# Router logits with stationary weights, and parked value operands split on VectorE, in a fused decoder-block kernel

## The chip, the core and the metric

The kernel runs on one NeuronCore of a Trainium2 chip. Its engines are TensorE (PE; loads of its stationary operand are listed apart, as PEld), VectorE (DVE), ScalarE (ACT), GpSimd (POOL) and SyncE (SP), which only issues DMAs; ACT and POOL issue some too. The metric is the device time of one execution in microseconds, lower is better.

## The reference, cut to what matters

The program is two layers over 16 x 128 tokens of width 512 (2048 tokens). Two of its parts are touched here: the mixture of experts of layer 0 and the value projection of layer 1's attention.

```python
ht = h.reshape(-1, d)                       # 2048 tokens x 512
logits = ht @ router_w                      # router_w: 512 x 8
probs = jax.nn.softmax(logits, axis=-1)
topv, topi = jax.lax.top_k(probs, K)        # K = 2 of 8 experts
...
sh = jax.nn.silu(ht @ sw_gate) * (ht @ sw_up) @ sw_down
...
v_img = (img_ctx @ vi_w + vi_b).reshape(B, -1, H, D)
```

## The kernel before

Products that need full precision are made in one of two ways. Most go through `three_passes` (L101 to L105): each operand is split into a lead, rounded to the format that TensorE takes in one pass, and a trail, which is the rest; three matmuls (lead by lead, lead by trail, trail by lead) make the product. The router logits do not: they are plain float32 matmuls. The profile lists every float32 matmul that is no transpose as two records, so the 64 matmuls of L1558 are 128 records.

The work is a sequence of phases with a barrier between them. Two phases are touched.

**Phase "shared"** (`turned_and_shared`). The 2048 tokens are four groups g of 512. For each group DVE writes the normalised rows (`stage_rows`, L1457), PE turns them in four column chunks c of 128 (`turn_rows`, L1550, four transposes a chunk), ACT moves each turned chunk out of PSUM twice, as `plain` and as `lead` (`turned_rows`, L1428 and L1429), and DVE makes the trail (L1470). `plain` has one buffer a chunk for all groups: ACT may write chunk c of group g only when the router's matmul over chunk c of group g-1 has been done. `route(g)` (L1558) takes 128 tokens of a chunk as the stationary operand (128x128) and streams the 8 router columns through it; so for each chunk there are four matmuls with 8 moving columns, and the logits come out with tokens on partitions. ACT keeps them (`keep_logits`, L1434). PE's order is turn 0, turn 1, route 0, turn 2, route 1, turn 3, route 2, route 3, and then the shared expert: `up(0)`, `up(1)`, `down_product(0)` and so on, all with 512 moving columns. When all logits are kept, DVE and ACT choose the experts (L1278 to L1329), PE counts in between (`counts`, L1335 and L1336, queued inside `up(0)` after 36 of its 48 matmuls), and POOL scatters the rows by indirect DMAs (L1486).

**Phase "routed"** (`routed_experts`). In its second half 39 tiles of 128 rows go through the experts' down projections. For each tile SP loads the hidden values, ACT makes their lead (`hidden_lead`, L1901), DVE their trail (`hidden_trail`, L1967, output `routed_ht`), PE does six matmuls (`down_product`), ACT copies the result out (L1910), and SP stores it. The loop over tiles is a hardware loop on DVE (`second`). Beside it POOL prepares operands for work that was deferred to the next phase, the "parked" ones: three sets k of four pieces of 128x512 (one of turned context, two of value weights). `park(k)` issues four loads behind waits on `down`, the count of finished tiles, and `cut_parked(k)` splits them: four TENSOR_SCALAR for the leads (L1810), then four TENSOR_TENSOR for the trails (L1814). PE uses the first products of them (32 + 32 + 32 matmuls in all) from the end of this phase on.

Of the kernel before, what the change touches and what calls it, by code (L numbers as in the profile page):

```python
# [16 lines left out]
F32 = mybir.dt.float32  # L17
# [3 lines left out]
ALU = mybir.AluOpType  # L21
# [6 lines left out]
C = D // P  # L28
GB = 4
# [1334 lines left out]
def turned_and_shared(nc, K, R, E1, lead, trail, normal, logits, rows_dram, gate_up_dram, rk, rk_dram):  # L1364
# [5 lines left out]
    with Phase(nc, "shared") as ph:  # L1370
# [7 lines left out]
        square = sb("square", [P, GB])  # L1378
        ms_done, rms_done, own_late = sem("ms_done"), sem("rms_done"), sem("own_late")
# [36 lines left out]
        def _(act):  # L1416
# [4 lines left out]
            def turned_rows(g):  # L1421
                for c in chunks(g):
# [8 lines left out]

            def keep_logits(g):
                act.wait_ge(logit_mm, (g + 1) * C)
# [12 lines left out]

# [94 lines left out]
        def _(pe):  # L1541
            def turn_rows(g):
                pe.wait_ge(staged, g + 1)
                for c in chunks(g):
# [9 lines left out]
            def route(g):  # L1554
                for k, c in enumerate(chunks(g)):
                    pe.wait_ge(lead_done, through(g, c))
                    for b in range(GB):
                        ins = nc.tensor.matmul(logit_bank(g)[:, b * E:(b + 1) * E], plain[:, c, b * S:(b + 1) * S],  # L1558
                                               E1.rw[:, c, :], start=(k == 0 and b == 0), stop=(k == C - 1 and b == GB - 1))
                    ins.then_inc(logit_mm, 1)  # L1560

            def up(u):
                cols = slice(u * N, (u + 1) * N)
                for f in range(FC):
                    if u:
                        pe.wait_ge(hid_done, 2 * u + f - 1)
                    else:
                        pe.wait_ge(logit_done, 3)
                    for bank, at in ((2 * f, 0), (2 * f + 1, UP)):
                        for c in range(C):  # L1570
                            w = slice(at + c * F + f * P, at + c * F + (f + 1) * P)
# [23 lines left out]
            turn_rows(0)  # L1595
            turn_rows(1)
# [14 lines left out]
def routed_experts(nc, K, R, E1, rows_dram, hid_dram, y_dram, weights, parked, parked_raw, ct_dram, v_w):  # L1611
# [10 lines left out]
    with Phase(nc, "routed") as ph:  # L1622
# [34 lines left out]
        parked_loaded = [sem(f"parked_loaded{k}") for k in range(1 + len(DEFERRED))]  # L1657
# [103 lines left out]
        def _(pool):  # L1761
# [40 lines left out]
            def park(k):  # L1802
                for c in range(C):
                    pool.wait_ge(down, 1 + k * 5 + c)
                    pool.dma_start(parked_raw[:, k, 1, c], parts[k][c]).then_inc(parked_loaded[k], 16)

            def cut_parked(k):
                pool.wait_ge(parked_loaded[k], 16 * C)
                for c in range(C):
                    nc.gpsimd.tensor_scalar(parked[:, k, 0, c], parked_raw[:, k, 1, c], 1.0, None, ALU.mult  # L1810
                                            ).then_inc(parked_lead, 1)
                for c in range(C):
                    pool.wait_ge(parked_lead, k * C + c + 1)
                    nc.gpsimd.tensor_tensor(parked[:, k, 1, c], parked_raw[:, k, 1, c],  # L1814
                                            parked[:, k, 0, c].bitcast(F32), ALU.subtract).then_inc(parked_trail, 1)
# [115 lines left out]
        def _(dve):  # L1931
# [63 lines left out]
            second(dve, hidden_trail, skip=2)  # L1995
# [1013 lines left out]
```

## Time and profile before

| what | value |
|---|---|
| median of 3 runs | 1477.15 us (1473.38 to 1482.09) |
| profiled execution, time | 1477.78 us |
| its span in the trace | 1476.1 us |
| busy: PE, DVE, ACT, POOL | 93%, 56%, 52%, 30% |
| mean granted TensorE clock | 0.953 of 2.4 GHz |
| router stage: first turn to the last logit matmul | 536.4 to 572.3 us |
| second half of "routed", tiles 10 to 23 | 806 to 844 us |

The span is cut into 40 slices of 36.9 us in the page; in a windows view each stretch has the busy time of every engine with the number of records, then the granted clock (1.00 is 2.4 GHz, 0.50 is 1.2 GHz), the busy share of the DMA engines and GB/s. A timeline row is start, duration (from the first start to the last end where several were merged), engine, line, operation, tiles, count, and in brackets the idle time of the engine before it with what ended it.

### The profile page before, as it was taken

To read this page: it belongs to the slowest core of one execution; us is meant where nothing else is said; L and a number is where in the kernel's file an instruction comes from. 1 tells how busy PE (TensorE), PEld (TensorE's weight loads), DVE (VectorE), ACT (ScalarE), POOL (GpSimd) and SP (SyncE) were. 2 spreads that over 40 slices of the span, in tenths; PEclk is the share of its full clock that TensorE was granted. 3 is DMA by queue.
4 is the path that set the end of the run, shared out by engine and by line. 5 is a ranking of instruction groups with operands and counts; after the bars stand their busy time and mean duration, and the time that the engine had idled before them with its cause. 6 is when DMAs were issued, how large, how long until landed. Compare 5 with 4: busy or idle time off the path is not lost. (4 is left out here: it accounts for less than half of the span.)

```text
span 1476.1 us, 24769 instructions
## 1 busy us (share of the span) xinstructions
PE 1366.5 (93%) x7406; PEld 1138.8 (77%) x7407; DVE 833.3 (56%) x1530; ACT 765.8 (52%) x1878; POOL 441.4 (30%) x411
## 2 busy tenths in 40 slices
PE   6899997999999879989998698999977999999998
PEld 5786676888788768868886476888866888888887
DVE  2443433476776775354444627754228877777866
ACT  3313234787878644134555254555438566665661
POOL 0110103354747300639923824211025400000032
PEclk9999995999999976999999799999989999999999
DMA  6998448887788401466657467655535555555413
GB/s 230 358 350 305 173 144 258 292 272 257 243 277 287 151 22 36 167 208 186 204 137 243 165 230 240 178 168 186 185 128 157 166 156 163 159 163 161 136 44 114
DMA packets 172983, 284.14 MB, mean 192 GB/s; under 512 B 30112, under 2 KB 64672, under 8 KB 172640
## 3 DMA queue, kind: packets, MB, share of 16 engines
q1 hardware_dynamic: 147088, 227.58, 48.7%
q0 software_dynamic: 8672, 29.37, 6.1%
q10 hardware_dynamic: 17136, 26.09, 4.8%
q8 instruction: 47, 0.77, 0.2%
q14 instruction: 40, 0.33, 0.1%
HBM read 176.29 MB, written 106.70 MB: 192 GB/s over the span
## 5 line engine op out<-in xcount | busy, mean ns | idle before, releaser
L2646 ACT ACTIVATE attend_prob<-banks,attend_row,rq 128x128 f32<-128x128 f32 x256 | 113.9, 455 | 51.9 <-DVE attend_row L2721 51.9
L103 PE MATMUL banks<-of_shared_split,heads_wl 128*128 128x512 f32 x256 | 108.8, 425 | 11.8 <-ACT heads_ksq L949 7.2
L103 PE MATMUL banks<-attend_wol,attend_ol 128*128 (+1 forms) x256 | 105.9, 414 | 0.0
L105 PE MATMUL banks<-of_shared_split,heads_wt 128*128 128x512 f32 x256 | 103.1, 403 | 0.0
L104 PE MATMUL banks<-of_shared_split,heads_wl 128*128 128x512 f32 x256 | 103.0, 402 | 0.0
L105 PE MATMUL banks<-attend_wol,attend_ot 128*128 (+1 forms) x256 | 100.6, 393 | 0.0
L103 PE MATMUL banks<-of_shared_split,of_ctx_lead 128*128 128x512 f32 x224 | 92.1, 411 | 9.1 <-DVE of_ctx_trail L425 5.3
L103 PE MATMUL banks<-queries_rows_split,queries_wl 128*128 128x512 f32 x256 | 100.4, 392 | 0.0
L105 PE MATMUL banks<-queries_rows_split,queries_wt 128*128 128x512 f32 x256 | 99.7, 389 | 0.0
L104 PE MATMUL banks<-attend_wot,attend_ol 128*128 (+1 forms) x256 | 99.7, 389 | 0.0
L104 PE MATMUL banks<-queries_rows_split,queries_wl 128*128 128x512 f32 x256 | 99.6, 389 | 0.0
L2628 POOL TENSOR_TENSOR x_kept<-x_kept,attend_tern_bias 128x512 f32<-128x512 f32 x12 | 15.5, 1294 | 264.4 <-ACT of_attend_raw L2684 262.8
L2336 DVE TENSOR_TENSOR queries_total<-queries_total,queries_sq 128x512 f32<-128x512 f32 x60 | 41.5, 692 | 86.9 <-ACT queries_sq L2264 86.9
L2260 ACT ACTIVATE queries_head<-banks,queries_bias 128x512 f32<-128x512 f32 x64 | 44.1, 689 | 87.6 <-PE banks L105 85.6
L105 PE MATMUL banks<-of_shared_split,of_ctx_trail 128*128 128x512 f32 x224 | 89.4, 399 | 0.0
L104 PE MATMUL banks<-of_shared_split,of_ctx_lead 128*128 128x512 f32 x224 | 88.8, 396 | 0.0
L897 ACT ACTIVATE heads_dec<-mlstm_gmax,mlstm_nat 128x128 f32<-128x128 f32 x264 | 83.2, 388 | 5.8 <-POOL mlstm_gmax L799 5.8
L1058 DVE TENSOR_TENSOR heads_total<-heads_total,heads_ksq 128x512 f32<-128x512 f32 x64 | 55.9, 874 | 53.6 <-ACT heads_ksq L949 53.5
L2659 ACT ACTIVATE attend_ol<-banks,of_attend_vbias 128x512 fp32r<-128x512 f32 x64 | 44.1, 689 | 69.5 <-PE banks L2851 69.5
L2745 DVE TENSOR_TENSOR x_kept<-x_kept,banks 128x512 f32 (+1 forms) x64 | 43.9, 686 | 61.4 <-PE banks L105 61.2
L1163 PEld LDWEIGHTS banks<-heads_ctx,heads_cmat 128*128 128x128 f32 x512 | 71.8, 209 | 8.6 <-POOL heads_ctx L808 3.1
L2832 PE MATMUL banks<-attend_kn,attend_q 128*128 128x128 f32 x512 | 69.8, 281 | 5.2 <-DMA attend_q<-q_heads 5.2
(353 smaller groups left out, 3707.5 us busy)
## 6 DMA issues: line engine op xcount, KB each, us to landing
mlstm_gmax<-running_max SPq DMA_DIRECT2D x36, 512.0 KB, 6.4
heads_raw<-in_L_xattn_ki_w SPq DMA_DIRECT2D x32, 512.0 KB, 6.6
k_heads<-heads_key ACTq DMA_DIRECT2D x64, 256.0 KB, 4.6
q_heads<-queries_head SPq DMA_DIRECT2D x64, 256.0 KB, 3.0
attend_q<-q_heads SPq DMA_DIRECT2D x64, 256.0 KB, 4.1
of_attend_k<-k_heads SPq DMA_DIRECT2D x60, 256.0 KB, 4.0
of_attend_v<-v_heads SPq DMA_DIRECT2D x60, 256.0 KB, 3.3
sorted_rows<-values_zeros SPq DMA_DIRECT2D x2, 5120.0 KB, 18.2
```

The lines of the kernel that those rows point to most:

```text
L103: nc.tensor.matmul(out, lead_l, lead_r, start=first, stop=False)
L104: nc.tensor.matmul(out, lead_l, trail_r, start=False, stop=False)
L105: return nc.tensor.matmul(out, trail_l, lead_r, start=False, stop=last)
L897: ins = nc.scalar.activation(dec[:, n % 2, b], gmax[:, h // 2 % 4, h % 2 * N + b * S:h % 2 * N + (b + 1) * S], ACT.Exp, scale=-1.0, bias=M ...
L1058: nc.vector.tensor_tensor(t, t, ksq[:, m % 2, :], ALU.add).then_inc(total_done, 1)
L1163: ins = nc.tensor.matmul(ps[:, n // 2 % 2, at:at + DH0 + 1], cmat[:, n % RING, b, :], ctx1[:, bass.ds(half(g), 1), b, n, :].rearrange("p a ...
L2260: nc.scalar.activation(head[:, u % HEADS_RING, :], ps[:, u % 4, :], ACT.Identity, bias=bias[:, h:h + 1]).then_inc(head_done, 1)
L2336: nc.vector.tensor_tensor(t, t, sq[:, u % 2, :], ALU.add).then_inc(total_done, 1)
L2646: ins = nc.scalar.activation(prob[:, j % 2, b, :], ps[:, j % 2, b * S:(b + 1) * S], ACT.Exp, bias=row[:, j % 2, 1, b:b + 1], scale=rq[:, b ...
L2659: nc.scalar.activation(ol[:, par, j, :], ps[:, 4 + j % 2, :], ACT.Identity, bias=vbias[:, bass.ds(quad_of(it) * 4 + j, 1)]).then_inc(ol_do ...
L2745: nc.vector.tensor_tensor(xb, xb, ps[:, 6 + b % 2, :], ALU.add).then_inc(acc_done, 1)
L2832: ins = nc.tensor.matmul(ps[:, j % 2, s], q[:, j, s], kn[:, j % 2, s], start=True, stop=True)
```

## The change

Two edits, in two phases.

In "shared", `route(g)` takes the 8 router columns of a chunk as the stationary operand (128x8) and streams all 512 tokens: one matmul a chunk, four a group. The logits then lie across, 8 partitions by 512 tokens. ACT copies them to SBUF (`keep_across`), four small transposes turn them upright (`upright_logits`) into the same bank, and `keep_logits` waits for those. The order on PE and ACT changes round this: the last chunk of a group is turned after the route of the group before; the uprights of groups 2 and 3 are put inside `up(0)`, after its first six matmuls.

In "routed", POOL only issues the twelve parked loads, piece by piece, one for every 2.5 tiles (`down` counts 1, 3, 6, 8, ... 28). DVE splits them: for a piece one TENSOR_SCALAR behind the hidden trail of tile 9 + 5*piece//2, and one TENSOR_TENSOR behind the next tile's. DVE's loop over tiles is written out.

```diff
@@ shared: ScalarE
+            def keep_across(g):
+                act.wait_ge(logit_mm, (g + 1) * C)
+                nc.scalar.activation(across[:, g % 2, :], logit_bank(g)[0:E, :], ACT.Copy).then_inc(across_done, 1)
...
-            turned_rows(0)
-            turned_rows(1)
-            keep_logits(0)
-            turned_rows(2)
-            keep_logits(1)
-            turned_rows(3)
-            keep_logits(2)
-            keep_logits(3)
+            first, rest = slice(0, 1), slice(1, C)
+            turned_rows(0, slice(0, C))
+            turned_rows(1, slice(0, C))
+            for g in range(2, G):
+                keep_across(g - 2)
+                turned_rows(g, first)
+                keep_logits(g - 2)
+                turned_rows(g, rest)
+            keep_across(G - 2)
+            keep_across(G - 1)
+            keep_logits(G - 2)
+            keep_logits(G - 1)
@@ shared: TensorE
-                    for b in range(GB):
-                        ins = nc.tensor.matmul(logit_bank(g)[:, b * E:(b + 1) * E], plain[:, c, b * S:(b + 1) * S],
-                                               E1.rw[:, c, :], start=(k == 0 and b == 0), stop=(k == C - 1 and b == GB - 1))
-                    ins.then_inc(logit_mm, 1)
+                    nc.tensor.matmul(logit_bank(g)[0:E, :], E1.rw[:, c, :], plain[:, c, :], start=k == 0, stop=k == C - 1
+                                     ).then_inc(logit_mm, 1)
+
+            def upright_logits(g):
+                pe.wait_ge(across_done, g + 1)
+                for b in range(GB):
+                    ins = nc.tensor.transpose(logit_bank(g)[:, b * E:(b + 1) * E], across[:, g % 2, b * S:(b + 1) * S],
+                                              K.ident[0:E, 0:E])
+                ins.then_inc(upright, 1)
...
+                            if u == 0 and f == 0 and at == 0 and c == 2:
+                                upright_logits(G - 2)
+                                upright_logits(G - 1)
...
-            turn_rows(2)
-            route(1)
-            turn_rows(3)
-            route(2)
-            route(3)
+            for g in range(2, G):
+                turn_rows(g, slice(0, C - 1))
+                upright_logits(g - 2)
+                route(g - 1)
+                turn_rows(g, slice(C - 1, C))
+            route(G - 1)
@@ routed: GpSimd
-            park(0)
-            for k in range(1, len(parts)):
-                park(k)
-                cut_parked(k - 1)
-            cut_parked(len(parts) - 1)
-            pool.wait_ge(parked_trail, len(parts) * C)
+            for piece in range(PIECES):
+                k, c = divmod(piece, C)
+                pool.wait_ge(down, 1 + 5 * piece // 2)
+                pool.dma_start(parked_raw[:, k, 1, c], parts[k][c]).then_inc(parked_loaded[piece], 16)
@@ routed: VectorE
-            second(dve, hidden_trail, skip=2)
+            def parked_piece(piece, part):
+                k, c = divmod(piece, C)
+                if part == 0:
+                    dve.wait_ge(parked_loaded[piece], 16)
+                    nc.vector.tensor_scalar(parked[:, k, 0, c], parked_raw[:, k, 1, c], 1.0, None, ALU.mult
+                                            ).then_inc(parked_lead, 1)
+                else:
+                    dve.wait_ge(parked_lead, piece + 1)
+                    nc.vector.tensor_tensor(parked[:, k, 1, c], parked_raw[:, k, 1, c],
+                                            parked[:, k, 0, c].bitcast(F32), ALU.subtract).then_inc(parked_trail, 1)
+
+            PARTS = {9 + 5 * piece // 2 + part: (piece, part) for piece in range(PIECES) for part in range(2)}
+            for n in range(2, TILES):
+                hidden_trail((n // 8, n % 8))
+                if n in PARTS:
+                    parked_piece(*PARTS[n])
+            dve.wait_ge(parked_trail, PIECES)
```

TensorE's program from the first turned rows to the shared expert, before (`of_x_normal` are the normalised rows, `of_ffn_raw` holds `plain`, `of_shared_rw` is the router's weight):

```order
L1550 MATMUL banks<-ident,of_x_normal 128x128 x32
L1558 MATMUL banks<-of_shared_rw,of_ffn_raw 128x8 x16
L1550 MATMUL banks<-ident,of_x_normal 128x128 x16
L1558 MATMUL banks<-of_shared_rw,of_ffn_raw 128x8 x16
L1550 MATMUL banks<-ident,of_x_normal 128x128 x16
L1558 MATMUL banks<-of_shared_rw,of_ffn_raw 128x8 x32
```

The same place now (`shared_hid` holds the logits that lie across):

```order
L1560 MATMUL banks<-ident,of_x_normal 128x128 x32
L1567 MATMUL banks<-of_ffn_raw,of_shared_rw 8x512 x4
L1560 MATMUL banks<-ident,of_x_normal 128x128 x12
L1573 MATMUL banks<-ident,shared_hid 128x8 x4
L1567 MATMUL banks<-of_ffn_raw,of_shared_rw 8x512 x4
L1560 MATMUL banks<-ident,of_x_normal 128x128 x16
L1573 MATMUL banks<-ident,shared_hid 128x8 x4
L1567 MATMUL banks<-of_ffn_raw,of_shared_rw 8x512 x4
L1560 MATMUL banks<-ident,of_x_normal 128x128 x4
L1567 MATMUL banks<-of_ffn_raw,of_shared_rw 8x512 x4
```

The 64 narrow router matmuls have become 16 wide ones; one chunk of groups 2 and 3 is turned behind a route, and four uprights stand ahead of routes 1 and 2.

VectorE's program in the second half of "routed", before, from the third tile to the head of its loop:

```order
L1967 TENSOR_TENSOR routed_ht<-routed_ring,routed_hl 128x256 x2
L1967 TENSOR_TENSOR routed_ht<-routed_lead,routed_hl 128x256 x4
L1967 TENSOR_TENSOR routed_ht<-routed_ring,routed_hl 128x256 x4
L1967 TENSOR_TENSOR routed_ht<-routed_lead,routed_hl 128x256 x3
```

The same place now, up to the third parked piece:

```order
L1970 TENSOR_TENSOR routed_ht<-routed_ring,routed_hl 128x256 x2
L1970 TENSOR_TENSOR routed_ht<-routed_lead,routed_hl 128x256 x4
L1970 TENSOR_TENSOR routed_ht<-routed_ring,routed_hl 128x256 x2
L2002 TENSOR_SCALAR parked<-parked_raw 128x512
L1970 TENSOR_TENSOR routed_ht<-routed_ring,routed_hl 128x256
L2006 TENSOR_TENSOR parked<-parked_raw,parked 128x512
L1970 TENSOR_TENSOR routed_ht<-routed_ring,routed_hl 128x256
L2002 TENSOR_SCALAR parked<-parked_raw 128x512
L1970 TENSOR_TENSOR routed_ht<-routed_lead,routed_hl 128x256
L2006 TENSOR_TENSOR parked<-parked_raw,parked 128x512
L1970 TENSOR_TENSOR routed_ht<-routed_lead,routed_hl 128x256 x2
L2002 TENSOR_SCALAR parked<-parked_raw 128x512
```

Each parked piece is two instructions behind two tiles' trails; there are 12 pieces, and the last tile has none behind it.

## Rows read from the trace of the kernel before

**Rows 1.** The page: granted TensorE clock in tenths, in 40 slices.
```profile
PEclk9999995999999976999999799999989999999999
```

**Rows 2.** Windows of the router stage: busy of PE, PEld, DVE, ACT, POOL, clock, DMA.
```profile
536.40:539.20 2.80, 2.72 (x13) 2.75 (x14) 2.33 (x7) 1.53 (x3) 0.00 (x0) 0.50 0.00 0
541.30:545.00 3.70, 3.70 (x35) 3.64 (x33) 3.23 (x7) 3.66 (x7) 0.00 (x0) 1.00 0.02 4
548.30:572.20 23.90, 23.81 (x113) 23.44 (x113) 6.98 (x12) 10.19 (x18) 0.00 (x0) 0.50 0.00 1
572.30:576.90 4.60, 4.60 (x12) 3.63 (x13) 3.04 (x28) 4.12 (x6) 0.00 (x0) 0.50 0.73 213
577.00:582.00 5.00, 5.00 (x23) 4.04 (x22) 4.03 (x34) 0.60 (x1) 0.00 (x0) 1.00 0.03 9
```

**Rows 3.** Timeline of PE's weight loads in the router stage.
```profile
541.29 3.65 PEld L1558 LDWEIGHTS banks<-of_shared_rw,of_ffn_raw 128*128 128x128 f32 x32
545.01 1.34 PEld L1550 LDWEIGHTS banks<-ident,of_x_normal 128*128 128x128 f32 x12
...
548.09 6.95 PEld L1558 LDWEIGHTS banks<-of_shared_rw,of_ffn_raw 128*128 128x128 f32 x32
```

**Rows 4.** Timeline of ACT in the router stage.
```profile
537.67 0.69 ACT L1428 ACTIVATE of_ffn_raw<-banks,of_ffn_wcol 128x512 f32<-128x512 f32 x1 [3.05 <-PE banks L1550]
...
547.02 0.25 ACT L1434 ACTIVATE of_x_logits<-banks 128x32 f32<-128x32 f32 x1
551.81 0.69 ACT L1428 ACTIVATE of_ffn_raw<-banks,of_ffn_wcol 128x512 f32<-128x512 f32 x1 [4.53 <-issue]
```

**Rows 5.** Timeline of PE in an earlier phase: wide float32 matmuls, small transposes.
```profile
116.66 3.65 PE L557 MATMUL banks<-mlstm_gmax,values_w_gate 128*64 128x512 f32 x8
120.24 0.51 PE L103 MATMUL banks<-of_shared_split,of_ctx_lead 128*128 128x512 f32 x1
...
133.26 0.43 PE L569 MATMUL banks<-ident,values_irow 32*128 32x32 f32 x4 [1.30 <-DVE of_ffn_raw L462]
```

**Rows 6.** Timeline at the expert choice: DVE's marks, PE's counts.
```profile
579.52 0.29 DVE L1295 TENSOR_TENSOR shared_both<-shared_chosen 128x128 f32<-128x128 f32 x1
...
582.84 0.38 PE L1335 MATMUL banks<-shared_both,shared_before 128*128 128x128 f32 x2
```

**Rows 7.** Timeline of DVE in the second half of "routed".
```profile
796.37 0.43 DVE L1967 TENSOR_TENSOR routed_ht<-routed_lead,routed_hl 128x256 fp32r<-128x256 f32 x1 [2.11 <-ACT routed_hl L1901]
...
805.95 1.22 DVE L1967 TENSOR_TENSOR routed_ht<-routed_ring,routed_hl 128x256 fp32r<-128x256 f32 x1 [1.07 <-ACT routed_hl L1901]
...
812.70 5.65 DVE L1967 TENSOR_TENSOR routed_ht<-routed_lead,routed_hl 128x256 fp32r<-128x256 f32 x2 [0.90 <-ACT routed_hl L1901]
...
844.15 0.43 DVE L1967 TENSOR_TENSOR routed_ht<-routed_lead,routed_hl 128x256 fp32r<-128x256 f32 x1 [2.31 <-ACT routed_hl L1901]
...
867.39 0.43 DVE L1967 TENSOR_TENSOR routed_ht<-routed_lead,routed_hl 128x256 fp32r<-128x256 f32 x1 [1.15 <-ACT routed_hl L1901]
```

**Rows 8.** Timeline of POOL there, and the parked loads' time to landing.
```profile
812.37 4.94 POOL L1814 TENSOR_TENSOR parked<-parked_raw,parked 128x512 fp32r<-128x512 f32 x4
...
DMA to landing us min/median/max: 3.7/5.2/6.3
```

**Rows 9.** Waits of PE from 806 to 842: us in total, times, longest.
```profile
PE banks L103 <- DVE routed_ht L1967: 13.2, 5, 5.1
```

**Rows 10.** Windows of the second half of "routed", and of the barrier behind it.
```profile
806.00:844.15 38.15, 24.81 (x79) 17.89 (x78) 24.80 (x13) 11.78 (x27) 35.50 (x29) 0.81 0.58 203
...
794.00:806.00 12.00, 11.55 (x46) 8.27 (x47) 2.86 (x8) 6.20 (x15) 3.02 (x6) 1.00 0.93 302
872.60:874.40 1.80, 0.01 (x1) 0.00 (x1) 0.00 (x0) 0.01 (x1) 0.00 (x0) 1.00 0.00 0
```

**Rows 11.** Groups of DVE instructions: count, busy us, mean ns.
```profile
L1470 DVE TENSOR_TENSOR of_x_trail<-of_ffn_raw,of_x_lead 128x512 fp32r<-128x512 f32 x16 | 10.9, 692 | 14.6 <-ACT of_x_lead L1429 14.6
L1457 DVE TENSOR_SCALAR of_x_normal<-x_kept,mv,of_shared_scale 128x512 f32<-128x512 f32 x16 | 7.9, 555 | 0.0
```

More of the change, by code:

```diff
@@ L1378, in turned_and_shared @@
         square = sb("square", [P, GB])
+        across = hid[0:E]
+        across_done, upright = sem("across_done"), sem("upright")
         ms_done, rms_done, own_late = sem("ms_done"), sem("rms_done"), sem("own_late")
@@ L1419, in _, with turned_rows @@
             act.wait_ge(E1.small_loaded, 32)
-            def turned_rows(g):
-                for c in chunks(g):
+            def turned_rows(g, at):
+                for c in chunks(g)[at]:
                     bank = ps[:, 4 * (g % 2) + c, :]
@@ L1430, in turned_rows @@
                                          ).then_inc(lead_done, 1)
+            def keep_across(g):
+                act.wait_ge(logit_mm, (g + 1) * C)
+                nc.scalar.activation(across[:, g % 2, :], logit_bank(g)[0:E, :], ACT.Copy).then_inc(across_done, 1)
             def keep_logits(g):
-                act.wait_ge(logit_mm, (g + 1) * C)
+                act.wait_ge(upright, g + 1)
                 nc.scalar.activation(logits[:, g * GB:(g + 1) * GB, :],
@@ L1541, in _, with turn_rows @@
         def _(pe):
-            def turn_rows(g):
+            def turn_rows(g, at):
                 pe.wait_ge(staged, g + 1)
-                for c in chunks(g):
+                for c in chunks(g)[at]:
                     if g >= 2:
@@ L1566, in up @@
                         pe.wait_ge(hid_done, 2 * u + f - 1)
-                    else:
-                        pe.wait_ge(logit_done, 3)
                     for bank, at in ((2 * f, 0), (2 * f + 1, UP)):
+                        if u == 0 and f == 0 and at:
+                            pe.wait_ge(logit_done, 3)
                         for c in range(C):
+                            if u == 0 and f == 0 and at == 0 and c == 2:
+                                upright_logits(G - 2)
+                                upright_logits(G - 1)
                             w = slice(at + c * F + f * P, at + c * F + (f + 1) * P)
@@ L1594, in _ @@
             pe.wait_ge(E1.small_loaded, 32)
-            turn_rows(0)
-            turn_rows(1)
+            turn_rows(0, slice(0, C))
+            turn_rows(1, slice(0, C))
             route(0)
-            turn_rows(2)
-            route(1)
-            turn_rows(3)
-            route(2)
-            route(3)
+            for g in range(2, G):
[4 more added lines that the diff above has]
+            route(G - 1)
             pe.wait_ge(trail_done, G * C)
@@ L1656, in routed_experts @@
         held_act, held_sp = sem("held_act"), sem("held_sp")
-        parked_loaded = [sem(f"parked_loaded{k}") for k in range(1 + len(DEFERRED))]
+        PIECES = (1 + len(DEFERRED)) * C
+        parked_loaded = [sem(f"parked_loaded{k}") for k in range(PIECES)]
         parked_lead, parked_trail, parked_product = sem("parked_lead"), sem("parked_trail"), sem("parked_product")
@@ L1800, in _ @@
             parts += [[v_w[c * P:(c + 1) * P, q * N:(q + 1) * N] for c in range(C)] for q, _ in DEFERRED]
[L1802 to L1815, printed above, removed]
-            park(0)
-            for k in range(1, len(parts)):
-                park(k)
-                cut_parked(k - 1)
-            cut_parked(len(parts) - 1)
-            pool.wait_ge(parked_trail, len(parts) * C)
+            for piece in range(PIECES):
+                k, c = divmod(piece, C)
+                pool.wait_ge(down, 1 + 5 * piece // 2)
+                pool.dma_start(parked_raw[:, k, 1, c], parts[k][c]).then_inc(parked_loaded[piece], 16)
         @block.scalar
```

## The prediction

> **What bounds the kernel now.** PE is busy 93% of the span, so I looked for the places where it is slow or stands. First the clock in 40 slices [rows 1]: most are 9; below it are the 7th (5) and the 31st (8), which the change does not touch, the 15th and 16th (7 and 6; 517 to 590 us) and the 23rd (7; 812 to 849 us). The two edits lie on these.
>
> *Router stage.* The windows [rows 2] show PE busy all the time, but from 548.3 to 572.2 at clock 0.50, that is 1.2 GHz; before, from 541.3 to 545.0, the same work ran at 2.4 GHz. The weight loads give the price [rows 3]: 16 router matmuls (32 records) took 3.65 us at full clock and 6.95 at half. Just before the clock fell PE had been doing this narrow work; it came back only after 4.6 us of the shared expert's wide matmuls [rows 2]. ACT waited 4.53 us for the slow route [rows 4], so PE bounds the stage.
>
> *Second half of "routed".* The DVE timeline [rows 7] lets one count tiles: from the trail of tile 10 (805.95) to that of tile 23 (844.15) are 13 tiles in 38.2 us, 2.94 each. From tile 23 to the last, tile 38 (867.39), are 15 in 23.24 us, 1.55 each; from tile 4 (796.37) to tile 10, six in 9.58 us, 1.60 each. In between one sees why: the trail that starts at 812.70 and its successor take 5.65 us where two take 0.85, and over the first of them lie POOL's four TENSOR_TENSOR, 4.94 us from 812.37 [rows 8]. PE waited for these trails 13.2 us in five waits [rows 9], and the whole stretch ran at clock 0.81 instead of 1.00 [rows 10]: after each long wait the clock was at half for some microseconds.
>
> **Edit 1, the parked operands.** It removes POOL's 24 splitting instructions, so nothing holds DVE's trails. At the neighbours' pace the 13 tiles take 13 x 1.55 = 20.2 us instead of 38.2, that is 18.0 less; tile 24 followed tile 23 still at half clock, which is about 1 us more (six matmuls of 0.22 us at full clock [rows 2], twice that at half). Gain 19.0 us. Ends: at 1.60 a tile 17.4 and no such 1 us; at 1.48 (the 15 tiles without that 1 us) 20.0.
>
> What it adds to DVE: 12 TENSOR_SCALAR, nearest row 0.56 us, and 12 TENSOR_TENSOR, nearest row 0.69 us [rows 11], one behind a tile's trail: 15 us in all. Their cover is DVE's wait for ACT in each tile, 1.07 to 1.15 us at full pace [rows 7]. 0.69 fits with some 0.4 left, so I take zero. Without that cover all 15 would lie on the path, since PE queues behind the trail; that is the upper end. Splitting instructions also wait for their load. Load k is issued when tile 1+k has been finished and used behind the trail of tile 9+k, which DVE makes about a tile ahead of PE: some 7 tiles, 11 us. The load landed in 3.7 to 6.3 us [rows 8], with the DMA engines at 0.93 [rows 10], and now the loads come one in 2.5 tiles and not bunched. So nothing waits. The last piece is cut behind tile 37, before PE needs it. POOL's wait on `down` holds nothing behind it but the next load.
>
> **Edit 2, the router.** Prices. A float32 matmul with 512 moving columns: four of them (8 records) stand between 116.66 and 120.24 [rows 5], 0.895 us each at full clock. 16 make 14.3 us, 3.58 a group, against 3.65 before at the same clock: so the edit saves nothing by the amount of work, only by the clock, if wide streams hold it up. Transposes: 12 in 1.34 us, 0.112 each [rows 3]. Four uprights: 0.43 us by four small transposes [rows 5]. ACT's pair for a chunk: eight pairs from 537.67 to 547.02, 1.17 each; so 0.6 for the copy across, which has as many columns, and 0.2 for keeping the upright ones [rows 4].
>
> The schedule by these, with the clock at 2.4 GHz, from where ACT ends its eighth pair (547.0). ACT copies across to 547.6; PE, which ended turn 2's three chunks at 546.3, makes the uprights to 548.1 and route 1 to 551.7. ACT may start group 2 when route 1's second matmul frees its chunk (549.9) and ends it, with one keep of 0.2, at 554.8; across to 555.4. PE ends turn 3's chunks at 553.5 and stands 2 us for that copy: a new wait. Uprights to 555.9, route 2 to 559.5, last chunk of turn 3 to 559.95. ACT's group 3 goes from 556.9 to 561.7; route 3 follows it closely and ends at 563.5. Before it was 572.2: 8.7 us less.
>
> Then the shared expert: it started with 4.6 us at half clock; at full clock 2.3 less. Inside `up(0)` come eight uprights, 0.9 more. The logits are now complete some 2.5 us after `up(0)` begins instead of 0.3. DVE needs 7.1 us from there to the counted marks (572.7 to 579.8 [rows 6]), so they come at +9.6; PE reaches the counts after 36 matmuls of 0.22 to 0.23 [rows 2] and the uprights, at +9.0: 0.6 us of wait, where it had 3 us to spare. The scatters start at about the same distance from `up(0)` as before, so nothing later is touched. Sum with the clock up: -8.7 - 2.3 + 0.9 + 0.6 = -9.5.
>
> The clock is the open point. At half clock a wide matmul costs 1.79 us, twice. What speaks for it staying up: the wide float32 matmuls of [rows 5] ran inside a dense stretch at full clock; the 1.8 us of idleness at a barrier left it at 1.00 [rows 10]; and turning alone, 2.8 us from 536.4, was enough to raise it (half there, full at 541.3, where the first route begins [rows 2, 3]). Against: the stage now has two pauses of 1.4 and 2 us, next to uprights that are as narrow as the old router matmuls. I reckon with one fall. It halves the speed of one route until wide work has raised it: route 2 would end at about 561.2 instead of 559.5, and the stage at 565.3, 1.8 us later. So edit 2 gives -9.5 with none, -7.7 with one; I take -8.5.
>
> The Trainium skill ("TensorE: Matmul & The Clock Gate", Part 4) says that transposes do not count as PE activity, by which the turning could never have raised the clock here; the rise with transposes alone before it says otherwise. By that rule the new stage, a third of it transposes, would tend to stay at 1.2 GHz, which is the second rival.
>
> **Sum.** The profiled execution took 1477.78 us, 0.6 above the median of the runs. 1477.8 - 19.0 - 8.5 = 1450.3; both phases end in barriers, and nothing of the later phases starts before them, so the gains stay. I predict 1450.
>
> **Rivals.**
> - *Only one of the covers holds: DVE's splitting shows.* If each of the 24 instructions delays the next trail and PE with it, by 0.2 us, 5 us are lost: 1455; all 15 would make 1465. For it: PE's slack over DVE is about half a microsecond a tile. Against: the cover of 1.1 us in every row of the quiet stretch. 0.12.
> - *The clock stays at 1.2 GHz through the router stage.* Three routes at 7.16 instead of 6.9, 16 uprights at 0.22, the shared expert's slow start as before, and the short stands for the copies: 0.8 + 3.5 + 1 = 5 us more than before instead of 8.5 less: 1478 - 19 + 5 = 1464. 0.08.
> - *Slower: the parked loads come late.* DVE's queue is in order, and a splitting instruction that waits for its load holds the trails of all later tiles. Each microsecond of landing beyond the 11 us costs one, twelve times; it makes the kernel slower when the loads take more than about 11 + 27.5/12 = 13.3 us each, and with loads of 14 us the time is 1478 - 27.5 + 36 = 1486. The rows show 6.3 at most, while DVE worked on the trails [rows 8]. The Trainium skill ("SBUF — State Buffer", "SBUF: two separate sides") says that a VectorE instruction which uses both ports of its one input, a float32 TENSOR_SCALAR among them, keeps GpSimd from writing descriptors. Here such an instruction lasts 0.56 us and comes once in 2.5 tiles, so it could add 0.56 to a landing, not 7. 0.03.
> - *Edit 1 does not do what it says:* the tiles are slow for the traffic on the DMA engines and not for POOL. Against it: PE's waits are for the trails, and the quick tiles before 806 ran at a DMA share of 0.93, the slow ones at 0.58 [rows 10]. Then only edit 2 is left: 1469. 0.04.
> - The forecast, both edits as above: 0.73.
>
> **How the numbers follow.** The forecast's own range is 1446 (1.48 a tile, no fall, no wait at the counts) to 1454 (1.60 a tile, two falls). To hold 8 in 10 the range takes in the better half of the other cases, and the spread of the runs (4 us either way): 1443 to 1461. A change of 0.5% (7.4 us) is about what this measurement can tell. All cases but the third end faster by more: faster 0.95; about the same 0.03 (two of the losses together); slower 0.02.
>
> **What would show it.** In the profile after: no POOL work from 780 us on but DMA issues; the trails at 0.42 us throughout, 1.5 to 1.6 us a tile, and no wait of PE for them; clock 1.00 from the third tile on. Router stage of about 27 us from the first turn to the last route, instead of 35.8; PE waiting for the copy across before the second set of uprights, about 2 us, and some tenths for the marks before the counts. Wrong would be: trails spaced wider just behind the splitting instructions; a clock of 0.50 through the routes; DVE waiting for a parked load.

## The result and the profile after

The changed kernel takes 1453.25 us (median; 1450.51 to 1455.23) against 1477.15 us (1473.38 to 1482.09): a ratio of 0.9832, 95% interval 0.9806 to 0.9858, or 24 us less. The profiled execution of after took 1450.51 us with a span of 1448.8. In a later comparison the same kernel gave 1450.64 and a ratio of 0.9827 (0.9793 to 0.986).

The page's line of the granted clock answers [rows 1]. The 16th slice went from 6 to 9 and the 23rd from 7 to 9. The 15th stays at 7: the first two groups are still turned at half clock in it. The 30th went from 8 to 6; it lies in a part that no edit touches.

```profile
PEclk9999996999999979999999999999969999999999
```

**Router stage.** PE's timeline, to be held against [rows 2, 3]; a row has start, duration, engine, line, operation, output and inputs, and what ended the wait before it:

```profile
534.08 6.51 PE L1560 MATMUL banks<-ident,of_x_normal 128*128 128x128 f32 x32 [6.58 <-DVE of_x_normal L1467]
540.52 3.60 PE L1567 MATMUL banks<-of_ffn_raw,of_shared_rw 128*8 128x512 f32 x8
544.05 1.53 PE L1560 MATMUL banks<-ident,of_x_normal 128*128 128x128 f32 x12
546.84 0.41 PE L1573 MATMUL banks<-ident,shared_hid 8*128 8x8 f32 x4 [1.26 <-ACT shared_hid L1436]
547.18 3.60 PE L1567 MATMUL banks<-of_ffn_raw,of_shared_rw 128*8 128x512 f32 x8
550.71 1.97 PE L1560 MATMUL banks<-ident,of_x_normal 128*128 128x128 f32 x16
554.43 0.41 PE L1573 MATMUL banks<-ident,shared_hid 8*128 8x8 f32 x4 [1.75 <-ACT shared_hid L1436]
554.77 3.60 PE L1567 MATMUL banks<-of_ffn_raw,of_shared_rw 128*8 128x512 f32 x8
558.30 0.66 PE L1560 MATMUL banks<-ident,of_x_normal 128*128 128x128 f32 x4
558.88 3.60 PE L1567 MATMUL banks<-of_ffn_raw,of_shared_rw 128*8 128x512 f32 x8
562.41 0.50 PE L103 MATMUL banks<-of_x_lead,of_shared_split 128*128 128x512 f32 x1
```

Every route (a group's four wide matmuls, eight records) lasts 3.60 us, the full-clock price, where route 1 of before took 6.95 at half clock [rows 3]. The two new waits stand where they were forecast, before the uprights, 1.26 and 1.75 us. From the first turn to the shared expert are 28.3 us, before 35.8. The windows say the same of the clock (columns: busy of PE, PEld, DVE, ACT, POOL, then clock, DMA share, GB/s):

```profile
543.00:548.00 5.00, 3.74 (x21) 1.89 (x20) 3.61 (x7) 3.79 (x7) 0.00 (x0) 1.00 0.00 0
548.00:553.00 5.00, 4.67 (x23) 2.18 (x21) 2.46 (x6) 3.85 (x8) 0.00 (x0) 1.00 0.01 3
553.00:558.00 5.00, 3.57 (x12) 0.96 (x12) 1.93 (x3) 3.50 (x8) 0.00 (x0) 1.00 0.00 0
...
796.00:838.00 42.00, 41.47 (x170) 30.44 (x169) 22.99 (x52) 25.52 (x57) 4.32 (x8) 1.00 0.93 318
```

**Second half of "routed".** The last of these windows answers [rows 10]: PE busy 41.5 of 42 us at clock 1.00, with the DMA engines at 0.93. In the DVE timeline the trails (L1970) and the new splitting (L2002, L2006) alternate, and DVE still waits for ACT before most of the trails:

```profile
795.73 0.42 DVE L1970 TENSOR_TENSOR routed_ht<-routed_ring,routed_hl 128x256 fp32r<-128x256 f32 x1 [0.68 <-ACT routed_hl L1904]
796.07 0.68 DVE L2006 TENSOR_TENSOR parked<-parked_raw,parked 128x512 fp32r<-128x512 f32 x1
797.20 0.43 DVE L1970 TENSOR_TENSOR routed_ht<-routed_ring,routed_hl 128x256 fp32r<-128x256 f32 x1 [0.44 <-ACT routed_hl L1904]
797.54 0.42 DVE L2002 TENSOR_SCALAR parked<-parked_raw 128x512 fp32r<-128x512 f32 x1
798.57 0.43 DVE L1970 TENSOR_TENSOR routed_ht<-routed_lead,routed_hl 128x256 fp32r<-128x256 f32 x1 [0.61 <-ACT routed_hl L1904]
```

The waits of [rows 9], 13.2 us in five, are gone. What is left of PE's waits for a trail between 760 and 845 us are two at the very start of the down projections (778.9 and 784.7 us), which the kernel before has too (16.4 us in seven from 760 us on, of which 3.2 are these two):

```profile
PE banks L103 <- DVE routed_ht L1970: 3.2, 2, 2.2
```

The parked loads landed in 3.6/5.2/7.3 us (least, median, most), and nothing waited for one.

To set executions side by side I use the time between landmarks of each trace. The *router stage* goes from PE's first turn to its first L103, the shared expert's first matmul; the *second half* from the first hidden trail to PE's first parked product behind the barrier. Stage and half are 35.8 and 86.7 us before, 28.3 and 66.4 after. The parts that no kernel here touches scatter by some us: what lies before the first turn took 529 to 539, what lies behind the half 602 to 607. So single profiles are compared by stretches, and whole times by medians or, between two comparisons, by the ratios to the kernel before, whose own median moved by 3 us from one to the next. The two measures differ by some us in places; then both are given.

### The profile page after: what moved, and what is told of

Read it like the earlier page. It is cut to its first block and busy times, and to the rows that moved or that the text cites. A ratio compares the mean times of both kernels' runs of the same rounds, so it can differ in the third digit from the quotient of the medians.

```text
span 1448.8 us, 24581 instructions
## 1 busy us (share of the span) xinstructions
PE 1351.7 (93%) x7326; PEld 1115.2 (77%) x7327; DVE 831.5 (57%) x1554; ACT 767.9 (53%) x1882; POOL 407.4 (28%) x387
## 5 line engine op out<-in xcount | busy, mean ns | idle before, releaser
L103 PE MATMUL banks<-of_shared_split,heads_wl 128*128 128x512 f32 x256 | 107.5, 420 | 11.1 <-ACT heads_ksq L949 6.0
L103 PE MATMUL banks<-attend_wol,attend_ol 128*128 (+1 forms) x256 | 105.9, 414 | 0.0
L103 PE MATMUL banks<-of_shared_split,of_ctx_lead 128*128 128x512 f32 x224 | 92.9, 415 | 9.2 <-DVE of_ctx_trail L425 5.2
L103 PE MATMUL banks<-queries_rows_split,queries_wl 128*128 128x512 f32 x256 | 100.5, 392 | 0.0
L2355 DVE TENSOR_TENSOR queries_total<-queries_total,queries_sq 128x512 f32<-128x512 f32 x60 | 41.5, 692 | 86.8 <-ACT queries_sq L2283 86.8
```

Of the source, the lines that this page charges most:

```text
L103: nc.tensor.matmul(out, lead_l, lead_r, start=first, stop=False)
```

## The experiments

All ran beside the kernel before: the first four with its median at 1474.77 us (15 runs), the next four at 1473.76 (25 runs), the last three at 1476.46 (11 runs).

### One edit at a time

The first kernel has the router edit alone (the parked code of before), the second the parked edit alone (the router code of before).

> Only the router edit; the parked operands are split by GpSimd as before. My theory: the router stage ends about 7.6 us earlier after its first turn and the shared expert starts at full clock, so 1477 - 8.5 = 1468.5 (1466 to 1471), with clock 1.00 through all four routes and the three long waits for routed_ht still there (13 us). Rival (the clock in the profiled execution was luck): the clock falls in one of the two pauses in this execution, and the gain is 5 us or less, 1472 or more.

> Only the parked edit; the router is as before. My theory: 13 tiles at 1.47 to 1.5 us instead of 2.94, and 1 us behind them: 1477 - 19.5 = 1457.5 (1455 to 1460). PE's waits for routed_ht fall from 13.2 us to none. If the two edits add up, the two gains of this run and of the router alone make 24 to 28 us. Rival (the two edits share a gain): this one alone already gives 1453.

Router alone: 1467.44 us (10 runs), ratio 0.9947 [0.9931 to 0.9964], 7.8 us less by the ratio. Parked alone: 1458.15 (6 runs), ratio 0.9889 [0.9867 to 0.9911], 16.4 us less. Together 24.2, which is what the change gains: within these intervals the edits add up.

The router-only trace did not keep the clock up in all four routes, as its theory had it: route 2 lasts 5.30 us, 1.7 more than the others. The gain was there all the same, and not the 5 us or less of the rival; its stage is 28.5 us. The parked-only trace has the narrow router in a second execution: stage 37.8 us, 2 more than before, with the clock down already in route 0 and no wait of PE after the first turn. PE's waits for a trail are the two at the start there, 3.2 us.

In the router-only trace the old rows are all there, 15.2 us in six, of which 4.7 in two are those of the start. PE's waits from 760 us to the end of the half, the trails on DVE, and GpSimd over them:

```profile
PE banks L103 <- DVE routed_ht L1986: 15.2, 6, 4.1
```

```profile
801.20 5.62 DVE L1986 TENSOR_TENSOR routed_ht<-routed_lead,routed_hl 128x256 fp32r<-128x256 f32 x2 [0.90 <-ACT routed_hl L1920]
```

```profile
800.85 4.94 POOL L1833 TENSOR_TENSOR parked<-parked_raw,parked 128x512 fp32r<-128x512 f32 x4
```

### What in the router kept the clock down: streaming little

This kernel undoes the router edit but for one thing: in the old form, tokens stationary, the eight router columns are streamed 16 times over. The logits are the same, only read with a stride. No copy across, no uprights, the old order.

```diff
-        ins = nc.tensor.matmul(logit_bank(g)[:, b * E:(b + 1) * E], plain[:, c, b * S:(b + 1) * S],
-                               E1.rw[:, c, :], ...)
+        ins = nc.tensor.matmul(logit_bank(g)[:, b * 16 * E:(b + 1) * 16 * E], plain[:, c, b * S:(b + 1) * S],
+                               E1.rw[:, c, :].unsqueeze(1).broadcast_to([P, 16, E]), ...)
```

> The parked edit, and the router as before in form and order: 128 tokens stationary, 64 matmuls; only the 8 router columns are streamed 16 times over (128 moving columns, 15 of 16 results unread). Weight loads are unchanged, and the longer stream (4 x 128 columns at 2.4 GHz are some 0.22 us by the 0.895 us of 512) fits under them. Theory (the loss was the clock alone, and it fell because PE streamed only 8 columns at a time): the clock stays at 1.00, each route takes 3.7 us, and the router stage is as short as with the change or up to 3 us shorter, for it has no copy across and no uprights: 1450 to 1454. Rival 1 (the clock follows the form of the work, loads of 128 columns against streams, and not how much is streamed): clock 0.50 through routes 1 to 3, time as with the parked edit alone, 1457 or more. Rival 2 (streams do not fit under the loads): clock 1.00 but routes of 5 us and more.

1448.0 us (6 runs), ratio 0.9826 [0.9798 to 0.9854]; stage 26.5 us. The time is 2 us better than the range of the theory, the stage within it. The comparison that isolates the columns is the one with the parked-only kernel, on the same chip: the two differ in nothing else, the time falls from 1458.15 us, with intervals of the ratios that do not touch, and the stage from 37.8. In the parked-only kernel the turning and the routing of a group from 539.41 us on went so:

```profile
539.41 3.65 PE L1550 MATMUL banks<-ident,of_x_normal 128*128 128x128 f32 x16
542.86 6.83 PE L1558 MATMUL banks<-of_shared_rw,of_ffn_raw 128*128 128x8 f32 x32
```

With the columns repeated:

```profile
544.48 0.63 PE L1550 MATMUL banks<-ident,of_x_normal 128*128 128x128 f32 x4 [1.07 <-ACT of_x_logits L1434]
544.94 3.74 PE L1558 MATMUL banks<-of_shared_rw,of_ffn_raw 128*128 128x128 f32 x32
548.52 1.47 PE L1550 MATMUL banks<-ident,of_x_normal 128*128 128x128 f32 x12
551.95 0.63 PE L1550 MATMUL banks<-ident,of_x_normal 128*128 128x128 f32 x4 [1.96 <-ACT of_x_logits L1434]
552.41 7.31 PE L1558 MATMUL banks<-of_shared_rw,of_ffn_raw 128*128 128x128 f32 x64
```

The same 32 weight loads take 3.74 us a group, as the 8-column form did at full clock (3.65, [rows 3]), and two groups in a row 7.31, so the clock no longer falls. The old form was not slow by itself: it hid its streaming under the weight loads, streamed next to nothing, and was then given half the clock. Sixteen times as many columns cost 0.09 us a group.

### How many columns, and in which order

Two more versions with repeated columns use a new order on PE, the route ahead of the last chunk's transposes:

```diff
 turn_rows(0); turn_rows(1); route(0)
-turn_rows(2); route(1); turn_rows(3); route(2); route(3)
+for g in range(2, G):
+    turn_rows(g, slice(0, C - 1))
+    route(g - 1)
+    turn_rows(g, slice(C - 1, C))
+route(G - 1)
```

> The kernel with the router's eight columns streamed 16 times (as in the earlier run of that name) and, besides, TensorE's program reordered there: the routing of the group before comes ahead of the last chunk's transposes, not behind them. That kernel showed two waits of TensorE for ScalarE's copy of the logits, 1.07 and 1.96 us, just ahead of that last chunk; behind 3.7 us of routing both should vanish. Theory: the stretch from the first turn to the shared expert goes from 26.5 to about 23.5 to 24.5 us, the clock stays up, and the median goes from 1448 to about 1445 to 1446. Rival (the routing then waits for ScalarE's leading parts, since ScalarE's pairs of 1.17 us are the bound of the stretch): no shorter, 26.5.

> The kernel with repeated router columns in the new order of TensorE, but with the eight columns streamed 4 times (32 moving columns) in place of 16 times (128). With 8 columns the granted clock fell to 1.2 GHz in the routing, with 128 it stayed up; the routing of a group lasted 3.65 and 3.74 us at full clock, so fewer columns save no time on TensorE. Theory A (what matters is how much the engine streams, and 32 columns are nearer to 8): the clock falls to 0.50 in part of the routing, the stretch from the first turn to the shared expert is 28 to 38 us. Theory B (32 columns suffice between the transposes): the clock stays at 1.00, 24 us, as with 128.

With 128 columns: 1444.36 us (1443.75 to 1444.89, 5 runs), ratio 0.9816 [0.9782 to 0.985], stage 24.1 us, and PE waits for nothing after the first turn. With 32 columns: 1454.32 us (4 runs), ratio 0.9851 [0.9804 to 0.9897], stage 28.0. Its clock fell twice, as these windows show, and the shared expert again began at half clock:

```profile
546.00:548.00 2.00, 2.00 (x20) 2.00 (x20) 2.00 (x5) 1.84 (x4) 0.00 (x0) 0.99 0.00 0
548.00:550.00 2.00, 2.00 (x12) 2.00 (x10) 1.24 (x3) 2.00 (x5) 0.00 (x0) 0.50 0.00 0
550.00:552.00 2.00, 2.00 (x15) 2.00 (x13) 1.16 (x2) 0.99 (x3) 0.00 (x0) 0.65 0.00 0
552.00:554.00 2.00, 2.00 (x21) 2.00 (x20) 0.50 (x1) 1.80 (x4) 0.00 (x0) 1.00 0.00 0
554.00:556.00 2.00, 2.00 (x16) 2.00 (x15) 1.07 (x3) 2.00 (x5) 0.00 (x0) 0.70 0.00 0
556.00:558.00 2.00, 2.00 (x11) 2.00 (x11) 1.20 (x2) 1.03 (x3) 0.00 (x0) 0.50 0.00 0
```

PE is busy 2.00 of 2.00 in each of them: an engine that never waits still lost its clock. That is theory A, at the short end of its stage of 28 to 38 us. Between the 32-column and the 128-column version only the number of streamed columns differs. The clocks rest on one profile each; the ratios point the same way, but their intervals overlap. (The clock had risen later in the turns of the 128-column trace, 6.59 us against 5.46; but the version before this one, also with 128 columns, had it early, two pauses besides, and no fall.)

### The pauses of the wide form

> The change with one edit: the four transposes that turn a group's logits upright stand between the second and the third wide product of the next group's routing, not ahead of the first. In the changed kernel TensorE waited 1.26 and 1.75 us ahead of these transposes for ScalarE's copy across (3.0 us over the stretch). Theory: 1.8 us of products now cover the copy; the waits vanish or shrink to under 0.5 us, unless the last chunk's transposes now wait for the copy back (up to 0.6 us each); the stretch goes from 28.3 to 25 to 26.5 us, the median 2 to 3 us below the change's. Rival (the stretch is bound by ScalarE's pairs of 1.17 us, 16 of them): it stays at 28.

```diff
 def route(g, inside=None):
     for k, c in enumerate(chunks(g)):
+        if k == 2 and inside is not None:
+            upright_logits(inside)
...
-    upright_logits(g - 2)
-    route(g - 1)
+    route(g - 1, g - 2)
```

1447.72 us (1442.35 to 1448.53, 6 runs), ratio 0.9794 [0.9759 to 0.9828]; stage 25.5. The change itself, beside it on the same chip:

> The change itself, unaltered, beside the others on one chip, so that the versions with repeated columns can be set against it. Expected: within 2 us of its median of 1453.25 us, a ratio to the kernel before of 0.983; the version with repeated columns in the new order (1444.36 us) is then some 8 to 9 us faster.

1450.64 us (1449.74 to 1453.73, 6 runs), ratio 0.9827 [0.9793 to 0.986]; stage 28.5. The ratio is the forecast one, the median 2.6 us lower than the first; so the version with 128 columns in the new order leads it by 6 us by the medians and by 2 by the ratios, and not by 8 to 9. The intervals of the two ratios overlap, but the runs on this one chip do not, and the traces show the 3 us. The waits of 1.26 and 1.75 us are gone in the version with the uprights inside:

```profile
544.04 1.88 PE L1569 MATMUL banks<-of_ffn_raw,of_shared_rw 128*8 128x512 f32 x4
545.85 0.41 PE L1575 MATMUL banks<-ident,shared_hid 8*128 8x8 f32 x4
546.19 1.88 PE L1569 MATMUL banks<-of_ffn_raw,of_shared_rw 128*8 128x512 f32 x4
```

The repeated trace of the change showed the fall of the clock that the prediction had reckoned with:

```profile
551.97 0.41 PE L1573 MATMUL banks<-ident,shared_hid 8*128 8x8 f32 x4 [1.75 <-ACT shared_hid L1436]
552.31 5.30 PE L1567 MATMUL banks<-of_ffn_raw,of_shared_rw 128*8 128x512 f32 x8
```

```profile
552.00:554.00 2.00, 2.00 (x7) 0.61 (x8) 0.24 (x1) 0.32 (x1) 0.00 (x0) 0.73 0.00 0
554.00:556.00 2.00, 2.00 (x4) 0.33 (x3) 0.69 (x1) 1.65 (x5) 0.00 (x0) 0.50 0.00 0
556.00:558.00 2.00, 2.00 (x8) 0.59 (x6) 0.69 (x1) 1.82 (x4) 0.00 (x0) 0.91 0.00 0
```

Seven profiles have this wide form with its two pauses. In five (router only, leads on GpSimd, lead six times, split earlier, the repeat) route 2 lasts 5.30 us; in two (the first profile of the change, trails on GpSimd) it lasts 3.60. In those two the clock had risen later in turns 0 and 1, which lasted 6.51 us against 5.03 to 5.64. So an execution pays once, either 0.9 to 1.5 us there or 1.7 us here, and the stages come out alike, 28.3 to 29.2. With the uprights inside, no route showed the fall, but that is one profile, in which turns 0 and 1 took 6.58; a fall averted by the missing pause is not shown by it.

### What blocked VectorE: GpSimd's operations of two inputs

Two kernels give GpSimd one half of the splitting back, one operation at a time between the loads.

> The changed kernel, but the leads of the parked pieces are made by GpSimd again (one TENSOR_SCALAR of 1.5 us a piece, spread out), the trails by VectorE. Theory (GpSimd's two-input TENSOR_TENSOR was what held VectorE for 4 to 5 us; its one-input instructions only stretch a trail from 0.42 to 0.8 us): within 2 us of the changed kernel, 1453 to 1456, trails of 0.8 us where they overlap, no wait of PE over 1 us. Rival (any GpSimd arithmetic blocks VectorE for its whole duration and puts PE behind): twelve stalls of about 1 us, 1462 or more.

> The mirror of the run with the leading parts on GpSimd: VectorE cuts the leading parts as in the change, GpSimd subtracts for the trailing ones, one at a time, spread out over the tiles and not four in a row. Theory A (a two-input operation of GpSimd holds VectorE's two-input operation for as long as it lasts, 1.2 to 1.3 us each): one or two of VectorE's trails beside each of the 12 subtractions last up to 1.3 us longer, which VectorE's idle 1.05 us mostly hides: time within 3 us of the change, stretched trails 0.43 to about 1.7 us in the trace. Theory B (it holds it through a whole batch only because four come in a row, and TensorE waits when VectorE is held for longer than about two tiles' slack): the same, and so 4.9 us stretches are gone. Rival C (any two-input subtraction on GpSimd costs several us each): 15 us slower or more, as with the kernel before.

Leads on GpSimd (TENSOR_SCALAR, one input): 1453.1 us (4 runs, 1449.55 to 1458.48), ratio 0.9848 [0.9815 to 0.9881], PE's wait for trails 3.2 us in the two at the start as in the change, half 69.5 us. A trail beside such an operation lasts 0.73 instead of 0.43 us (the first one 1.22), which the idle time hides:

```profile
808.13 0.73 DVE L1980 TENSOR_TENSOR routed_ht<-routed_lead,routed_hl 128x256 fp32r<-128x256 f32 x1 [0.98 <-ACT routed_hl L1914]
```

```profile
808.48 1.73 POOL L1825 TENSOR_SCALAR parked<-parked_raw 128x512 fp32r<-128x512 f32 x1
```

Trails on GpSimd (TENSOR_TENSOR, two inputs): 1460.73 us (10 runs), ratio 0.992 [0.9894 to 0.9947], half 77.0 us. DVE and GpSimd there:

```profile
806.80 1.90 DVE L1981 TENSOR_TENSOR routed_ht<-routed_lead,routed_hl 128x256 fp32r<-128x256 f32 x1 [2.01 <-ACT routed_hl L1915]
```

```profile
807.12 1.29 POOL L1825 TENSOR_TENSOR parked<-parked_raw,parked 128x512 fp32r<-128x512 f32 x1
```

DVE's trail had begun at 806.80, 0.3 us before GpSimd, and ended at 808.70, 0.3 us after it: its own 0.42 us, the whole 1.29 of the other, and 0.2 more. From 796 to 850 us PE waited for such trails:

```profile
PE banks L103 <- DVE routed_ht L1981: 8.0, 9, 1.2
```

The mechanism is theory A's, but its "mostly hidden" was wrong: 8.0 us of waits for 12 subtractions, 0.7 each; the time is 7 to 10 us above the change by the medians and 13 by the ratios. Four in a row, as before the change, are worse (5.1 us at a time), yet one alone already costs.

### How far the covers reach

> The change with each of the 12 leading parts that VectorE cuts of the parked pieces cut six times over, each time waiting for the one before (the same numbers are written; the result is unchanged). It prices the cover. A TENSOR_SCALAR of this size lasts 0.42 us in the changed kernel, so one piece costs VectorE 5 x 0.42 or about 2.1 to 2.6 us more, in one tile, against an idle wait for ScalarE of about 1.05 us in a tile. Theory (VectorE's splitting is free only as far as its idle time reaches): per piece 2.1 to 2.6 plus the first 0.42, less about 1.05 of that tile and some lead over TensorE, leaves 1 to 1.9 us on the path, times 12: 12 to 22 us slower than the change, about 1466 to 1475. Rival (the stage is bound by the transfers at a 0.93 share, and VectorE has slack over several tiles, which it wins back between pieces): under 4 us slower than the change.

> The change with each parked piece split behind the trail of tile 3+k instead of tile 9+k (k = 0, 2, 5, 7 ...), its load still issued when tile 1+k is finished. It prices the rival of late loads. In the changed kernel a piece is split some 12.2 us after its load's issue (782.4 to 794.6 us), and the loads land in 3.6 to 7.3 us. Six tiles of about 1.5 us earlier leave 3.2 us. Theory (VectorE's queue is in order, so a splitting instruction that waits for its load holds the trails behind it): each waits about 2 to 3 us, some 1 us of it in VectorE's idle time, 12 times: 12 to 25 us slower than the change, with VectorE shown waiting for the transfer of parked_raw. Rival (the wait is taken up by tiles finished ahead): under 4 us slower.

With each lead cut six times DVE has some 2.2 us more in every 2.5 tiles: 1464.12 us (10 runs), ratio 0.9938 [0.9912 to 0.9963], 11 to 13 us above the change by the medians and 16 by the ratios, where 12 to 22 were forecast; half 80.2 us. PE's waits from 794 to 845 us, none of which the change has:

```profile
PE banks L103 <- DVE routed_ht L1970: 10.2, 10, 1.3
```

Up to 860 us they are 12.4 us in twelve, one for each piece: of the 2.2 us, 1.2 were hidden. So DVE's slack is about one tile's idle wait, as forecast, and not several tiles'.

With the pieces split six tiles earlier DVE waits for their loads, and the time is 1459.64 us (8 runs), ratio 0.9905 [0.9876 to 0.9934], 6 to 9 us above the change by the medians and 11 by the ratios; half 74.8 us, in a profiled execution of 1454.32 us. DVE's waits from 790 to 842 us:

```profile
DVE parked L2002 <- DMA parked_raw<-in_L_xattn_vi_w: 15.0, 8, 2.7
DVE routed_ht L1970 <- ACT routed_hl L1904: 13.0, 12, 1.5
DVE parked L2002 <- DMA parked_raw<-ctx_turned: 3.6, 2, 2.3
```

PE waited 7.0 us in that stretch (794 to 842) for the trails queued behind. The mechanism is the theory's; the size, 12 to 25 us, was too high: 18.6 us of DVE's waiting reached PE as 7 in that execution, which was 5 us faster than the median.

## Why the prediction was right

The forecast of 1450 us lies 3 us below the measured 1453.25. By its own steps:

*Edit 1 takes the block away.* Right, and now shown by experiment. The trails last 0.42 to 0.43 us each, the pace from tile 10 to tile 23 is 1.47 us (13 tiles from 795.73 to 814.85) where 1.55 was taken, and the clock is 1.00. The rival that traffic was the cause is out: the loads are the same, the DMA share rose to 0.93, and the two kernels with one half of the splitting on GpSimd issue them as the change does; with the leading parts there PE's waits are as short as in the change, with the subtractions there they are back, 8.0 us.

*Its size, 19.0.* Mis-sized: the parked edit alone measured 16.4, with 17.4 as the lower end named; by its interval it may be 13 to 20. The profiles point the same way. The half lasts 86.7 and 84.5 us in the two with GpSimd's splitting as before, and 66.4 to 70.1, mean 68.6, in the eight with both parts on DVE or the leads alone on GpSimd (lead six times, split earlier and trails on GpSimd apart): some 17 us. The step read its price and its pace from one execution, and this stretch scatters by 3 us even between two of the changed kernel (66.4 and 69.2). That the rest is this scatter is argued, not shown. Who sets only the two profiles of before and after side by side is misled: their spans differ by 27.3 us, almost the forecast 27.5, because the one of after happens to have the shortest half of the eight.

*DVE's added work costs nothing.* Right. Behind a subtraction 0.35 to 0.9 us of idle wait were left. The instructions lasted 0.42 and 0.68 us; the first was priced at 0.56. The six-fold lead shows where the cover ends.

*The loads come in time.* Right: 12.2 us from issue to use at the first piece (11 were reckoned), landing in 7.3 at most. A delay of GpSimd's issues by VectorE's splitting, for which the prediction allowed 0.56 us a landing, does not show in the issues (0.54 us) or in the median landing (5.2 us), both as before; the longest landing rose from 6.3 to 7.3. The rival's price, one us per us late, twelve times, was too high: 18.6 us late cost PE 7 in the profile, and 6 to 11 us of time.

*Edit 2 gains only by the clock.* Right: 3.60 a group against 3.65, clock 1.00 but for the one fall in five of the seven profiles. The rival of a stage at 1.2 GHz is out. Forecast for the schedule: 27 us from the first turn to the last route, with none or one fall; measured 28.3, since the clock rose 1.4 us later in the turns. The waits came at 1.26 and 1.75 us (1.4 and 2.0 were forecast), the one at the counts at 0.3 (0.6), route 2 with a fall at 1.7 longer (1.8). In all 7.8 us by the experiment (5 to 10 by its interval), 8.5 forecast.

*The range.* Its low end of 1446 does not follow from the cases named for it: 1477.8 less 20.0 and less 10.1 (8.7 and 2.3 gained, 0.9 lost) is 1447.7. Nothing else hangs on it. The slice of 8 in [rows 1] is the 30th, not the 31st.

*The rise with transposes alone.* In the changed kernel too PE did nothing but turn until the clock rose, within the 6.51 us from 534.08 (0.50 up to 539, 1.00 from 540 us on); the next rows, at full rate, are the routes. The Trainium skill's rule ("TensorE: Matmul & The Clock Gate", Part 4), that transposes do not count as activity, again disagrees with the trace.

What the prediction did not see is that the clock could be had without the wide form: it took the weights' change of place and the columns streamed for one thing, and only the second mattered.

## What to carry to other kernels

A matmul that is bound by its weight load streams almost nothing, and PE may be given half its clock while it reads as fully busy, as here with 8 and with 32 columns. Before the operands change places, try streaming the same few columns repeatedly under the load. Here 16 times over cost 0.09 us a group and, with the new order, made the shortest router stage, 24.1 us against 25.5 of the wide form with its pauses filled and 28.3 of the change. By whole times the first two cannot be told apart: the medians of 1444.36 and 1447.72 us come from different comparisons, and by the ratios, 0.9816 and 0.9794, the order is the other way round; those of the change, 0.9832 and 0.9827, have intervals that overlap with both, though on their one chip the wide form with its pauses filled was 3 us faster than the change. A subtraction on GpSimd is not free beside VectorE: put its two-input operations where VectorE's queue is not on PE's path, or give them to VectorE when it waits anyway. Price a cover in idle time per tile, and check it by making the hidden work larger.

## What the runs showed of the hardware

- Clock and streamed columns: the same loop of 32 weight loads a group kept 2.4 GHz with 128 moving columns (3.74 us), and fell to 1.2 GHz in places with 32 (one route 6.87 us) and with 8 (6.95 us, and 6.83 in the parked-only kernel). With 32, and with 8 in the parked-only kernel, PE had not waited since its first turn; with 128 in the old order it waited twice, 1.07 and 1.96 us, and kept the clock. The turning between the routes did not save it.
- In the wide form a pause of 1.75 us and the uprights behind it are followed by a fall in five of seven profiles and by none in two, the two in which the clock had risen late. When the clock falls and rises thus differs between executions of the same code, and the time lost came out about the same.
- GpSimd's operation of two inputs (128x512 float32, 1.29 us) holds up a two-input operation of VectorE for its whole length, also one whose row had begun 0.3 us before (0.42 us became 1.90). Its one-input operation makes it 0.3 us longer, once 0.8. GpSimd's own TENSOR_SCALAR takes 1.5 us, and 1.7 beside such an operation, for what VectorE does in 0.42.
